# Attention on one Trainium2 core: the products with V and with ones placed in one group in every step

## The reference

```python
q = (x @ wq).reshape(B, S, H, hd).transpose(0, 2, 1, 3)
...
scores = jnp.einsum('bhqd,bhkd->bhqk', q, k) / jnp.sqrt(jnp.asarray(hd, x.dtype))
causal = jnp.tril(jnp.ones((S, S), dtype=bool))
scores = jnp.where(causal, scores, jnp.finfo(x.dtype).min)
attn = jax.nn.softmax(scores, axis=-1)
ctx = jnp.einsum('bhqk,bhkd->bhqd', attn, v)
```

## Time and profile before

| what | us |
|---|---|
| median of three runs (lowest, highest) | 2467.4 (2467.37, 2468.62) |
| the profiled execution's own time | 2469.27 |
| its span, first to last instruction | 2467.3 |
| PE busy, whole span | 2368.8 |
| DVE / ACT / POOL busy, whole span | 1214.5 / 824.9 / 860.7 |
| mean granted TensorE clock, share of full speed | 0.987 |
| the softmax attention, start to end | about 301 to 915 |

### The profile page before, as it was taken

The page is one execution under the profiler, slowest core; times in us unless marked ns, Lnnn a source line. Parts: engine busy times, 40 slices in busy tenths (PEclk is TensorE's granted clock), DMA queues, the critical chain, the costliest instruction groups (busy, mean ns, idle before and its releaser), DMA issues. The chain is left out here.

```text
span 2467.3 us, 39742 instructions
## 1 busy us (share of the span) xinstructions
PE 2368.8 (96%) x12645; PEld 1777.9 (72%) x12645; DVE 1214.5 (49%) x2553; ACT 824.9 (33%) x1392; POOL 860.7 (35%) x1097
## 2 busy tenths in 40 slices
PE   7999899999999999899999996999999999999997
PEld 5888755555555547688888885788888878888886
DVE  3334477777777758522222216686764732222221
ACT  3222255555555542344444432011111212222221
POOL 2000055655656552233333333533424212222211
PEclk9999999999999999999999998999999999999999
DMA  6886335445454428512121014140403242222200
GB/s 239 280 294 214 116 91 141 116 116 133 116 137 116 116 70 290 155 38 52 34 51 34 35 35 141 52 147 24 170 34 138 91 117 52 51 51 51 54 32 34
DMA packets 265536, 262.50 MB, mean 106 GB/s; under 512 B 127986, under 2 KB 161778, under 8 KB 264948
## 3 DMA queue, kind: packets, MB, share of 16 engines
q1 hardware_dynamic: 249556, 217.39, 30.6%
q0 software_dynamic: 6400, 25.26, 3.3%
q10 hardware_dynamic: 9504, 18.88, 2.2%
HBM read 168.68 MB, written 92.27 MB: 106 GB/s over the span
## 5 line engine op out<-in xcount | busy, mean ns | idle before, releaser
L177 DVE CUSTOM_DVE_ANT_0 junk<-psum,causal 128x896 bf16<-128x896 f32 (+7 forms) x512 | 373.6, 751 | 170.6 <-PE psum L887 146.4
L996 ACT ACTIVATE p_probs<-psum 128x512 f32<-128x512 f32 (+1 forms) x640 | 317.9, 555 | 276.2 <-PE psum L900 270.6
L1506 POOL TENSOR_TENSOR p_h_lo<-p_h,p_h_hi 128x512 fp32r<-128x512 f32 x128 | 164.4, 1284 | 307.9 <-ACT p_h_hi L1531 307.9
L900 PE MATMUL psum<-qst,kst 98*128 98x512 f32 (+3 forms) x768 | 224.0, 371 | 6.4 <-POOL p_ones L739 5.9
L789 POOL TENSOR_SCALAR_AFFINE_SELECT p_probs<-p_probs 128x128 f32<-128x128 f32 x512 | 141.5, 298 | 229.1 <-ACT p_probs L996 225.8
L2270 ACT ACTIVATE p_h<-psum,ffn_b 128x512 f16<-128x512 f32 x128 | 88.0, 688 | 375.9 <-PE psum L1164 360.0
L900 PEld LDWEIGHTS psum<-qst,kst 98*128 98x128 f32 x768 | 132.3, 191 | 111.9 <-DVE rowmax L177 42.7
L2251 POOL CAST p_h<-p_h 128x512 fp32r<-128x512 f16 x128 | 83.7, 654 | 368.1 <-ACT p_h L2270 367.6
L1164 PE MATMUL psum<-ffn_xT,la_w_hi 128*128 128x512 f32 x512 | 200.2, 391 | 8.7 <-POOLq L63 5.8
L887 PE MATMUL psum<-kst,qst 96*128 96x128 f32 (+3 forms) x720 | 208.5, 364 | 0.0
L1560 PE MATMUL psum<-tern,p_h_hi 128*128 128x512 f32 x512 | 199.4, 389 | 1.7 <-POOL p_h_lo L1506 1.7
(11 more groups left out here) (239 smaller groups left out, 4800.1 us busy)
## 6 DMA issues: line engine op xcount, KB each, us to landing
qst<-q_parts SPq DMA_DIRECT2D x96, 256.0 KB, 4.8
kst<-k_parts SPq DMA_DIRECT2D x96, 256.0 KB, 6.9
q_parts<-p_qk_out SPq DMA_DIRECT2D x32, 512.0 KB, 3.4
k_parts<-p_qk_out SPq DMA_DIRECT2D x32, 512.0 KB, 3.2
p_x<-in_x_t POOLq DMA_DIRECT2D x8, 1024.0 KB, 8.4
v_rows<-p_v_out SPq DMA_DIRECT2D x32, 256.0 KB, 4.0
v<-v_rows SPq DMA_DIRECT2D x16, 512.0 KB, 4.2
attention_out<-p_o_out SPq DMA_DIRECT2D x32, 256.0 KB, 2.1
```

The costliest lines, as they stand in the source:

```text
L177: return dve.tensor_tensor_reduce(view(junk[:, 0:n]), bank, view(self.causal[:, SEQ - n:SEQ]), 1.0, FLOOR, ALU.add, ALU.max, self.rowmax[: ...
L900: mm = pe.matmul(psum[:, bank, col:col + CH - q0], kst[s][0:KD + 2, g, j * P:(j + 1) * P], qst[s][0:KD + 2, c, g, q0:CH], start=True, stop ...
L996: act.activation(probs[:, n % 2, g, col:CH], psum[:, banks_of(s, "s", st)[0], col:CH], ACT.Exp, scale=SM_SCALE).then_inc(p_ready, 1)
L1506: pool.tensor_tensor(h_lo[:, m % 2, :], h[:, m % 2, :], f32(h_hi[:, m % 2, :]), ALU.subtract).then_inc(hl_done, 1)
```

## The change

Only the texts in `STEPS` change. In steps 4, 5 and 7 other pieces stood between "v" and "o"; now the two letters are neighbours in all ten. The entries and scores are spread anew: entries by step were 9, 3, 3, 3, 3, 3, 2, 4, 2, 2 and are 10, 1, 5, 2, 3, 0, 3, 4, 4, 2. In five steps some pieces now stand behind "vo" (0, 2, 4, 6 and 7; before it was 2 alone, besides those between "v" and "o"). Numbers, shapes and operands of all instructions stay; the banks of the ring, the waits on them and DVE's order follow from the texts. DVE's division of the first half still begins before entry 18; that of the second begins before entry 8 and not 9.

```diff
-    STEPS = [([(0, 0)], "seseeseeeeseevo"), ([(0, 1), (0, 3)], "sesessevo"),
-             ([(0, 2)], "eeesssvos"), ([(1, 0)], "esesssevo"),
-             ([(1, 1)], "ssesveseo"), ([(1, 2)], "sssveeseo"),
-             ([(1, 3)], "sseessvo"), ([(1, 4)], "sesseveseo"),
-             ([(1, 5), (1, 7)], "ssessevo"), ([(1, 6)], "ssessevo")]
+    STEPS = [([(0, 0)], "eeseeseseeevosee"), ([(0, 1), (0, 3)], "sesssvo"),
+             ([(0, 2)], "eseeeessvos"), ([(1, 0)], "ssessevo"),
+             ([(1, 1)], "ssesevose"), ([(1, 2)], "ssssvo"),
+             ([(1, 3)], "seesevoss"), ([(1, 4)], "esssseevoe"),
+             ([(1, 5), (1, 7)], "ssesseeevo"), ([(1, 6)], "sseessvo")]
```

## The result

**The time.** The changed kernel takes 2473.36 us in the median of 16 runs (2471.77 to 2474.74), the kernel before 2467.98 in 16 runs beside them (2467.1 to 2468.84): ratio 1.0021, interval 1.0014 to 1.0027. It is 5.4 us slower, just over the 0.2% named as the bound; the forecast was 2466.0, no change. The profiled execution of after is the shortest of its 16 (2471.77 us) and that of before (2469.27) lies above all 16 of its own, so the spans differ by 2.5 us only. The stages show more: the attention lasts 613.9 us before and 618.8 after, +4.9, while the start and the rest of this one execution are 0.5 and 1.8 shorter.

What follows compares the result with a forecast made beforehand. PE's stream was taken as the bound. A unit: 38.45 - 0.99 - 0.70 + 1.75 = 38.51, +0.9 us over 15; last unit -2.2; so 2467.4 - 1.3 = 2466 us, range 2455 to 2476, likeliest case 2462.5 to 2471.

Steps and rivals of the forecast that it cites:

- the 0.2% named as the bound: Whole kernel: the measurement can tell 0.2%, 4.9 us, from no change; the forecast of staying within it got 0.45.
- What bounds: Steady attention units: PE issues almost without a pause, busy 38.38 of 38.45 us, so its own stream sets the time.
- The three splits, -0.99: Steps 4, 5 and 7: pieces between v and o cost 0.33 us a split; closing three saves 0.99 a unit.
- The waits that come from DVE, 1.75: New order: PE waits for banks until DVE reads maxima, in steps 7 to 9, 0 and 2; 1.75 us a unit.
- The waits that go, -0.70: Old pauses in step 0 (0.43) and step 6 (0.25) vanish because their places are rewritten; 0.7 us a unit.
- 15 units at +0.06, +0.9: Steady units: each goes from 38.45 to 38.51 us, so 15 of them add 0.9 us.
- DVE, POOL, ACT, SP at nothing: Attention units: rebuilt DVE order, later exponentials, SP's loads and POOL's masks were costed at nothing.
- the cover I named: PE's work of one step, some 3.5 us, hides late loads; without it each would show one for one.
- My list of scores behind a group: Two scores of step 6 and one of step 0 go behind groups; their exponentials come 2 to 3 us later.
- The last unit, -2.2: Last unit: splits go (1.0), transpose waits about 0.5 less, a wait near the last groups loses 0.7; ends -1 and -3.
- The first, smaller waits: Rival: a unit's new waits only equal the old 0.7, giving 2450 us, or 2458 if half way; chance of either 0.33.
- The second, DVE the bound from step 7 on: Rival: entries 30 and 31 wait for DVE too, some 0.6 us a unit more, giving 2475 us; chance 0.22.

Runs made afterwards that it cites:

- experiment 2: Changed kernel with v moved up in steps 4, 5 and 6, putting three splits back, entries and scores in the same sequence: 2486.61 us, ratio 1.0078.
- Experiment 3: Kernel before with DVE's maxima of all entries taken over the first 128 keys only: 2465.89 us, ratio 0.9993.
- experiment 4: Changed kernel with DVE's maxima of all entries taken over the first 128 keys only: 2450.54 us, ratio 0.9936.
- Experiments 11 to 14: Kernel before respread, ten closed groups: two spreads, step 9's last score behind vo (2480.5, 2471.03 us); second, then first, with it ahead (2463.28, 2475.74 us).
- (5): Also written experiment 5: changed kernel with POOL's three folds of the last unit moved behind all masks: 2472.23 us, ratio 1.0017.
- experiment 8: Kernel before with entries and scores respread, three splits kept but in steps 6, 7 and 8, short entries in steps 0 and 1: 2459.22 us, ratio 0.9963.
- experiment 6: Changed kernel with v of step 7 moved ahead of the fourth score, putting one split in: 2468.95 us, ratio 1.0005.

## Why the prediction failed

Step by step, in its own order. The forecast was -1.3 us and the runs say +5.4. By the two profiles 4.1 us of the gap of 6.7 lie in the 15 units (+5.0 for +0.9) and 2.1 in the last one (-0.1 for -2.2).

**What bounds: right.** PE's stream stayed the path. No other engine is busy for more than 30.0 of 38.86 us.

**The three splits, -0.99: right.** 0.92 for three in experiment 2, 0.94 between experiments 3 and 4.

**The waits that come from DVE, 1.75: right.** By distances against experiment 4, entry 25 waits 0.47 (forecast 0.6), the third score of step 8 0.71 (0.7), step 9 0.29 (0.2), step 2 0.17 (0.1), step 0 nothing (0.15): 1.64. Of the 0.47, 0.19 goes over to the "v" right behind once DVE's work is cut, so experiment 4 gives back a little less than the sum of these waits, 1.51.

**The waits that go, -0.70: here it failed.** I took out 0.43 in step 0 and 0.25 in step 6 as tied to places that are rewritten, and put nothing of their kind into the new order. Experiment 3 says that they were not DVE's: with DVE's maxima cut, the old unit loses 0.17 us only, and its steps 0 and 6 stay at 3.65 and 3.96. Experiment 4 against 3 says that such pauses did not go: without DVE's share the new unit is 0.94 shorter, and the three splits alone are worth 0.92 to 0.99. So the pauses that are not DVE's are as large in the new order as in the old, within 0.05. The balance of a unit is -0.94 (splits and other pauses) + 1.51 (DVE's waits in after) - 0.17 (DVE's waits in before) = +0.40, as measured, where I had -0.99 + 1.75 - 0.70 = +0.06: 0.58 too much taken out, 0.24 of it hidden by too much put in. Two different things had been set against each other: pauses measured in the old order, whatever their cause, and one cause walked in the new. Like against like, DVE's waits alone (1.75 by the walk, 0.17 in the old order) would have given +0.59 a unit and, with the -2.2 of the last unit, 2474. To come so near the measured 2473.4 would have been luck in part: 2.9 us too much in the units against 2.1 too little in the last one. Which engine owns each of the smaller pauses stays open.

**15 units at +0.06, +0.9: measured +5.0.** Thirteen at 0.40 are 5.2, the first adds 0.1, and the last steady one takes 0.3 off.

**DVE, POOL, ACT, SP at nothing: right here, and one letter away from wrong.** In after no wait for a DMA stands on PE. Experiments 11 to 14 show that the cover I named is lost once the last score of step 9 stands behind the group, since the loads wait for its exponential: 5.4 and 6.5 us of waits, gone with the letter moved back. In after it stands ahead of the group. My list of scores behind a group leaves out the one of step 4; no wait of PE in that step is in the timeline. The price is not the late load alone but what is queued behind it on SP, which I had not named.

**The last unit, -2.2: failed, -0.11.** The transpose's wait fell from 0.77 to 0.28, as forecast. Up to step 9 the unit is 1.3 us ahead, of the 1.5 that this and the splits were to bring; step 9 gives 1.2 of it back. "POOL's chain stays as it is, and I let 0.7 of the wait go": a chain that stays as it is is the reason why the wait does not go. PE reaches the last masked product but one earlier and waits 1.44 us instead of 1.07. That the wait of the earlier trace rows was put down to an exponential misled me; the product needs masks too, and in the kernel before they end at 912.23, where it starts at 912.38. With the folds moved in both kernels that wait is nearly gone; in (5) waits for exponentials stand in step 9 in its place, and the two units are within 0.22 of each other.

**The rivals.** The first, smaller waits, is out: DVE's new waits are 1.64 by distances, near the 1.75 and far from the 0.7 that it asked for. The second, DVE the bound from step 7 on, had the right side and near the right time (2475) with a mechanism that the trace does not show: entries 29 to 31 follow each other at 0.46 and 0.49, against 0.47 and 0.46 with DVE's work cut, and DVE is idle twice between 646 and 652. The Trainium skill (TensorEngine Tiling (Array Packing), PSUM Bottleneck) says that packing does not speed up the reading of PSUM. Here that shows in single places and not in the average: with DVE at 77% of the unit its waits take back more (1.51 us) than the closed groups gave (0.94) in after, and in the spread of experiment 8, at 81%, no wait of PE for DVE is in the list.

## What to carry to other kernels

A group of matmuls that needs no bank is also the time in which the engine that frees the banks catches up; before closing groups to save switches, see what then stands close together; a split that fills a wait for a wide read can pay for itself (experiment 6). When two orders are compared, walk both by the same rule: pauses measured in the old order can't be set against one cause walked in the new. And a letter's place also sets when the loads queued behind it are issued: follow the queue to its last entry.

## What the runs showed of the hardware

- The fold of 128x512 on POOL (L770) takes 1.28 us in experiment 5, 1.74 in the kernel before and 2.27 in after, the same instruction beside different work. Which neighbour stretches it was not tried.
- PE's wait of 1.44 us before the last v but one was followed by full clock in after and by a granted clock of 0.51 for 3.34 us in experiment 6, though PE was idle for nearly the same share of the 2.1 us ahead of it in both. What decides was not tried.
- A piece that had to wait for its bank also makes the next one late. From its start to the next start the score at 645.86 takes 0.34 us, and 0.24 in experiment 4, where it does not wait; entry 33 takes 0.57 for 0.46, entry 25 0.46 for 0.35. The prediction had 0.1 for it.
- Cutting DVE's work in a unit nearly to half (30.00 to 16.88 us in after) is worth 22.8 us in after and 1.9, not clear of the noise, in the kernel before, though in both PE is busy for over 98% of the unit.
- The same read by DVE starts 0.94 us after the matmul in the hardware loop and 0.71 behind it, and in after the unit is 0.8 us longer for it.
